# A mixture-of-experts stage whose row gathers are issued less far ahead: tokens four tiles instead of eight, results two token tiles instead of four, and additions spread more evenly over the steps

## The reference

```python
def _moe_forward(hidden_states, ...):                  # 1792 tokens x 256
    shared = einsum('ti,hi->th', silu(x @ sh_gate_w.T) * (x @ sh_up_w.T), sh_down_w)
    probs = softmax(x @ router_weight.T)
    top_v, top_i = top_k(probs, 2)
    ...
    for e in range(8):
        gate, up = split(x @ gate_up_proj[e].T)        # 176 columns each
        out = out + (silu(gate) * up @ down_proj[e].T) * combine[:, e:e + 1]
    return out + sigmoid(x @ shared_gate_w.T) * shared
x = _layernorm(x + attention(x))
x = _layernorm(x + cross_attention(x, ctx))
x = _layernorm(x + _moe_forward(x, ...))
```

## Time and profile before

| | |
|---|---|
| time, median of 3 runs | 1758.07 us (1757.87 to 1758.46) |
| span of the profiled execution, its own time | 1772.4 us |
| PE busy | 1696.6 us, 96% of the span |
| DVE, ACT, POOL busy | 1226.0, 932.4, 662.2 us |
| mean granted TensorE clock | 0.985 |
| chain that ended last | PE 77%, DVE 3%, DMA 3%, issue 2% |
| indirect fetches of tokens | 35, at 1608.7 to 1680.3 us |
| indirect gathers of results | 28, at 1708.5 to 1753.2 us |

### The profile page before, as it was taken

The page is one execution under the profiler, slowest core; times in us unless marked ns, Lnnn a source line. Parts: engine busy times, 40 slices in busy tenths (PEclk is TensorE's granted clock), DMA queues, the critical chain, the costliest instruction groups (busy, mean ns, idle before and its releaser), DMA issues.

```text
span 1772.4 us, 28874 instructions
## 1 busy us (share of the span) xinstructions
PE 1696.6 (96%) x10034; PEld 1525.3 (86%) x10034; DVE 1226.0 (69%) x3381; ACT 932.4 (53%) x1707; POOL 662.2 (37%) x417
## 2 busy tenths in 40 slices
PE   6999789999999999999999999999999999997986
PEld 6788678999898998989898989899898989887975
DVE  4555367777877768787777777776878787565446
ACT  4433246565656555565656565555556565543532
POOL 1111063333434435343333343443534331435334
PEclk9999999999999999999999999999999999999998
DMA  5133563333232324252333323233424221432322
GB/s 191 52 116 113 179 125 83 44 87 64 62 66 61 67 74 77 60 96 42 86 44 87 66 61 66 62 66 80 75 62 91 42 55 20 99 110 62 114 76 84
DMA packets 103000, 140.36 MB, mean 79 GB/s; under 512 B 37038, under 2 KB 81872, under 8 KB 102736
## 3 DMA queue, kind: packets, MB, share of 16 engines
q1 hardware_dynamic: 60928, 115.53, 27.3%
q10 hardware_dynamic: 38912, 14.80, 4.7%
q0 software_dynamic: 3024, 8.26, 1.7%
HBM read 113.68 MB, written 24.89 MB: 78 GB/s over the span
## 4 chain that ended last, share of the span: by engine, by line
PE 77%; DVE 3%; DMA 3%; issue 2%; ACT 1%; another core or an unknown queue 1%; POOL 0%; ACTq 0%; POOLq 0%; DVEq 0%; SPq 0%
PE b_turn L758 16%; PE b_out L775 9%; PE b_out L777 9%; PE b_out L776 9%; PE b_score L744 8%; PE b_score L746 8%; PE b_score L745 8%; PE b_out L785 5%; PE c_gate L1410 2%; DMA rden_store<-b_rden 2%; PE c_down L1437 1%; PE c_up L1424 0%; DVE c_up L1728 0%; DVE b_p L897 0%
## 5 line engine op out<-in xcount | busy, mean ns | idle before, releaser
L815 ACT CAST b_pT_hi<-b_turn 125x512 fp32r<-125x512 f32 (+1 forms) x768 | 406.3, 530 | 546.2 <-PE b_turn L758 543.8
L911 DVE TENSOR_TENSOR b_pT_lo<-b_turn,b_pT_hi 125x512 fp32r<-125x512 f32 (+1 forms) x768 | 477.8, 623 | 268.4 <-ACT b_pT_hi L815 262.9
L897 DVE CUSTOM_DVE_ANT_0 b_p<-b_score,b_mask_add 128x500 f32<-128x500 f32 x672 | 451.2, 673 | 56.6 <-PE b_turn L758 24.0
L758 PEld LDWEIGHTS b_turn<-ident,b_p 128*125 128x125 f32 x2688 | 409.9, 186 | 57.6 <-issue 1.1
L758 PE MATMUL b_turn<-ident,b_p 128*125 128x128 f32 x2688 | 418.5, 272 | 0.8 <-ACT b_p L821 0.8
L821 ACT ACTIVATE b_p<-b_p,b_shift 128x1500 f32<-128x1500 f32 x224 | 347.4, 1551 | 16.2 <-DVE b_top_min L905 8.3
L775 PE MATMUL b_out<-b_pT_hi,b_c_hi 125*128 125x512 f32 (+1 forms) x768 | 346.8, 452 | 7.2 <-DVE b_pT_lo L911 7.2
L1034 POOL TENSOR_TENSOR b_oT_lo<-b_oT,b_oT_hi 128x896 fp32r<-128x896 f32 x32 | 67.8, 2120 | 622.1 <-ACT b_oT_hi L843 622.1
L776 PE MATMUL b_out<-b_pT_lo,b_c_hi 125*128 125x512 f32 (+1 forms) x768 | 281.2, 366 | 0.0
L777 PE MATMUL b_out<-b_pT_hi,b_c_lo 125*128 125x512 f32 (+1 forms) x768 | 281.2, 366 | 0.0
L744 PE MATMUL b_score<-b_cT_hi,b_q_hi 128*128 128x500 f32 x672 | 264.6, 394 | 9.5 <-DVE b_cT_lo L984 9.5
(11 more groups left out here) (248 smaller groups left out, 2408.8 us busy)
## 6 DMA issues: line engine op xcount, KB each, us to landing
cT_in<-in_ctxT SPq DMA_DIRECT2D x32, 750.0 KB, 11.7
b_c_in<-in_ctx SPq DMA_DIRECT2D x32, 750.0 KB
q_store<-a_fold_in_or_q_stage SPq DMA_DIRECT2D x16, 896.0 KB, 4.0
q_in<-q_store SPq DMA_DIRECT2D x32, 448.0 KB, 8.2
b_rden_all<-rden_store ACTq DMA_DIRECT2D x32, 256.0 KB, 4.4
b_rden_all<-rden_store ACTq DMA_DIRECT2D x32, 192.0 KB, 4.6
b_mask_in<-in_mask SPq DMA_DIRECT2D x32, 187.5 KB, 10.7
slot_store<-c_y2T SPq DMA_DIRECT2D x35, 128.0 KB, 1.7
```

The costliest lines, as they stand in the source:

```text
L758: mm = pe.transpose(turn_bank[n % 3][0:CK, u * 128:(u + 1) * 128], p[slot % 2][:, u, c * CK:(c + 1) * CK], ident[:])
L815: act.copy(pT_hi[:, n % 3, 0:w], turn_bank[n % 3][0:CK, 0:w]).then_inc(hi_done, 1)
L897: dve.tensor_tensor_reduce(out=p[slot % 2][:, u, keys], in0=score_bank[j][:, 0:FW], in1=mask_add[:, b, keys], scale=1.0, scalar=-3.0e38, o ...
L911: dve.tensor_tensor(pT_lo[:, n % 3, 0:w], turn_bank[n % 3][0:CK, 0:w], pT_hi[:, n % 3, 0:w].bitcast(F32), ALU.subtract).then_inc(lo_done, 1)
```

## The change

A fetch now waits until the tile four before it is transposed, where it waited for the one eight before; there are still eight buffers. A gather now waits for the additions of the token tile two before it, where it waited for the one four before. The tuple of additions per step is (0, 1, 1, 1, 2, 1, 1, 2, 1, 1, 1, 1), where it was (0, 1, 1, 2, 2, 2, 1, 0, 1, 1, 1, 1); its sum stays 13, and the fourteenth addition follows the last step.

```diff
-        X_DEEP, Y_DEEP = 8, 4
+        X_DEEP, Y_DEEP, X_AHEAD, GATHER_AHEAD = 8, 4, 4, 2
...
-        COMBINE_AT = (0, 1, 1, 2, 2, 2, 1, 0, 1, 1, 1, 1)
+        COMBINE_AT = (0, 1, 1, 1, 2, 1, 1, 2, 1, 1, 1, 1)
...
             def fetch_x(s):
                 if s == 0:
                     pool.wait_ge(route_chain, SOURCED)
-                if s >= X_DEEP:
-                    pool.wait_ge(x_turned, s - X_DEEP + 1)
+                if s >= X_AHEAD:
+                    pool.wait_ge(x_turned, s - X_AHEAD + 1)
                 pool.indirect_dma_start(out=x_in[:, s % X_DEEP, :], out_offset=None, in_=D["y2"],
...
             def gather(k):
                 n = ORDER[k]
-                if k >= GATHERS:
-                    pool.wait_ge(added, 2 * (k - GATHERS + 1))
+                if k >= GATHER_AHEAD:
+                    pool.wait_ge(added, 2 * (k - GATHER_AHEAD + 1))
                 for j in range(2):
```

## The result

| | before | changed |
|---|---|---|
| time, median of 14 runs each | 1756.88 us (1754.39 to 1760.85) | 1761.22 us (1759.05 to 1765.19) |
| ratio | | 1.0025, 95% interval 1.0017 to 1.0033 |
| span of the profiled execution | 1772.4 us | 1757.5 us |

The change costs 4.3 us; 1755.6 had been forecast, a gain of 2.5. The time lies in the stated range, on the side of the slower rival. The profiled executions say the opposite of the timed ones: there the changed kernel is 14.9 us faster. A run's time is its span plus 1.8 us (1759.32 and 1757.5 for the changed kernel's profiled run), so the profiled execution of before stood for some 1774 us, and none of the timed runs of that kernel, then or later, was over 1763.65.

The account below looks back on a forecast made before the run. Bound by TensorE, with two holes (some 15 us) blamed on unbroken runs of indirect DMAs on GpSimd. Fetches -3.0, gathers and additions -5.3 + 4.8 + 1 = +0.5: -2.5 us, so 1755.6 us; range 1749 to 1764.

Parts of the forecast that it names:

- the slower rival: Step 17 to the end: holes don't come from the runs of DMAs, or timed runs lack them; 1766.8 or about 1763; chance 0.22.
- its two holes: TensorE's pauses near tile 9 of the routed stage and at 1720 to 1732 us, second shared stage; together some 15 us.
- Part 1, the fetches: Routed stage: fetches four ahead end their run earlier, so TensorE goes on sooner after tile 9; -3.0 us.
- Part 2, the order up to addition 5: Second shared stage: VectorE is the limit and addition 5 ends at 1731.4 instead of 1736.7; -5.3 us.
- Part 2, from addition 5 to the last three tiles: Second shared stage: a new chain over GpSimd takes 30.4 us where it was 25.6; +4.8 us.
- the three legs over GpSimd: Waits for gather 7 and a scale, gathers 9 and 10 and a scale, and gather 13: 6.1, 8.6 and 4.8 us.
- The tail: From addition 11's end to the last three tiles: 5.8 us where it was 3.7, 2.1 of the +4.8.
- +1 for the first six DMAs: Start of the gathers: the first six DMAs are still nearly one unbroken run, so some instruction starvation stays; +1 us.
- The rival of timed runs without holes: Variant of the slower rival: only the +4.8 and the old order's faster start count; about 1763; chance within its 0.22.
- so here it was not hidden: Near 1722 to 1732 us: no instruction-queue packets while TensorE crawled, taken as instruction loads kept waiting by gathers.

Follow-up runs that it names:

- the first profile: The kernel before, unchanged, in the profiled execution that the prediction read: span 1772.4 us, routed stage 99.84 us, second shared stage 53.77 us.
- e1: The kernel before, unchanged, run and profiled again: 1755.84 us, ratio 0.9997; profiled span 1755.3 us, second shared stage 46.68 us.
- e8: The kernel before with eight semaphores for gathers, so gathers run up to eight token tiles ahead instead of four: 1758.36 us, ratio 1.0008.
- e9: The kernel before, unchanged, profiled once more with one run: 1758.20 us; profiled span 1756.4 us.
- e10: The kernel before, unchanged, profiled yet again with one run: 1756.30 us; profiled span 1754.5 us.
- e2: The kernel before with only the fetches held to four tiles ahead; gathers and additions as before: 1756.24 us, ratio 0.9993.
- e5: The changed kernel with the scales of tiles 0 to 3 and 4 to 6 computed behind gathers 5 and 8 instead of 7 and 10: 1758.09 us, ratio 1.0015.
- e6: As e5, and the last two gathers wait for the additions four tiles before: 1756.55 us, ratio 1.0004 to the kernel before.
- e3: The kernel before with only the gathers held to two tiles ahead; fetches and additions as before: 1760.29 us, ratio 1.0016.
- e4: The kernel before with only the additions moved; fetches eight ahead, gathers four: 1759.38 us, ratio 1.0000.
- e7: The changed kernel with gathers three token tiles ahead instead of two: 1757.11 us, ratio 1.0003 to the kernel before.

## Why the prediction was wrong

**The step that failed is the first one**, "its two holes (together some 15 us) come from how far ahead GpSimd runs", and with it the assumption that they are there in every run. The observation was right: engines stood still, and the profile names nothing in the kernel that they waited for. The step from there to a lack of instructions was not: no run shows it, and the loads of the first profile lie where those of e1 lie. That the holes lay inside runs of DMAs doesn't show a cause: e1, e8, e9 and e10 have as long or longer runs without them. The number that spoke against it was in the table: the profiled span was 14.3 us over the median of runs that agreed within 0.6 us. I named this in a rival and gave it too little weight. The holes were as large as that difference, and this should have settled it.

**Part 1, the fetches: -3.0 forecast, 0 measured** (e2: 0.9993, interval to 1.0002; routed stage 92.06 against 92.50). That a fetch four ahead is early enough was right; the gain was the hole's. The sum had a slip as well: 2.3 us, the landing counted from the issue's end, was added to the start of the fetch at 1638.46. With the 3.26 us of the earlier trace rows its transfer ends at 1641.7 and that of fetch 13 at 1638.0, so silu 9 could have come some 0.4 us earlier, not 1.1.

**Part 2, the order up to addition 5: -5.3 forecast.** Counted from the first gather, addition 5 was forecast to end at 1731.4 - 1708.55 = 22.85 us. It ended at 1718.30 - 1695.52 = 22.78. That it fits to 0.07 us is partly luck: addition 1 ended 9.61 us after the first gather, not 9.34, and the walk from there took 13.17 us, not 13.5. The walk was sound; the thing it was compared with was not. In e1 the same addition ends 21.07 us after the first gather, not 28.15, so the term is **+1.7**: the addition now stands one step later in the program.

**Part 2, from addition 5 to the last three tiles: +4.8 forecast, +3.6 measured.** The chain was forecast at 30.4 us and took 1747.47 - 1718.30 = 29.17; in e1 it took 25.61, the 25.6 of the first profile. The holes of the first profile lay ahead of addition 5, so this stretch of it was sound. The 1.2 us too many lie nearly all in the three legs over GpSimd: 6.1, 8.6 and 4.8 us were forecast, and 5.6, 8.3 and 4.4 measured. ScalarE's waits, 2.2 and 3.2 us, came where they were put. The tail, "now 5.8" where it was 3.7, took 5.45 us and has VectorE wait 1.76 us for the last gather, and e5 and e6 show that scales and tail together are nearly all of the cost.

**+1 for the first six DMAs, "still nearly one run": 0.** No run shows such a term; the walk up to addition 5 came out without it.

With the right baseline the same walk gives 22.85 + 30.4 - 46.68 = +6.6 us, where the traces have +5.3 and the runs +4.3 (3.0 to 5.8 by the interval). The rival of timed runs without holes had put the time at about 1763; it came to 1761.22.

The Trainium skill (Runtime: NRT & Kernel Launch, section Instruction fetch mechanics) says that crossing a block of instructions is mostly hidden. The trace of e8 agrees, in which a load landed within a run of sixteen gathers without a pause, and so does the first profile, with its load at 1710 us. My "so here it was not hidden" did not follow: a window with no load in it doesn't show a load that stopped an engine.

## What to carry to other kernels

- Compare the profiled span with the timed runs before reading a stall in it. If the difference is as large as the stall, the profile shows an execution that isn't the one being timed: profile again before explaining it.
- Before a prefetch is held back, count what else stands behind it on its in-order queue. In the changed kernel the rows themselves were in time but for the first and the last gather; it was the small computation queued behind the gathers (1.6 us of work) that came late and held up ScalarE, and through it VectorE and TensorE. Moving it ahead won back 3.2 of 5.3 us. With the additions in their old steps (e3) the same queue made a gather's rows late instead.
- Look-ahead can have an edge: here three tiles cost nothing that shows (1.0003), two cost 0.25%. I read the edge, and this is not shown, as the point where issue and landing of a pair of gathers (2.5 us, and 3.3 from the second's issue), plus what is queued behind them, outgrow the steps until their use.

No version beat the kernel before. What TensorE still waits for in its second shared stage is VectorE, as e1's waits from 1690 us on show, and gathers eight ahead (e8: 1.7 and 1.8 us) don't change that:

```profile
PE c_up L1356 <- DVE c_h_lo L1734: 1.8, 2, 1.5
...
PE c_down L1376 <- DVE c_y L1750: 1.8, 1, 1.8
```

## What the runs showed of the hardware

In one of the twelve profiled executions of this study, ScalarE, VectorE and TensorE crawled at two places, for some 7 and some 10 us, with no wait in the program to account for it, and TensorE's granted clock fell to the lower of its two levels in both (1640.0 to 1646.8 and 1725.3 to 1735.6 us). Against e1 the two stages took 7.3 and 7.1 us longer. The cause stays open.

The clock also fell in executions without a hole. In the second shared stage it was at its lower level for 6.8 us in the changed kernel, behind TensorE's wait of 3.1 us, and for 3.4 us in e1 (from 1731.6 us), behind one of 1.8; in e4, e6 and e7 it fell only within the stage's last 1 us. What this costs no run separates: in the changed kernel's chain TensorE has no part there, in the chains of e3 and e9 it has.

Back-to-back indirect DMAs, one of 128 rows every 1.25 us, go on beside full matmul streams without slowing them: in e1 a tile took 2.1 to 2.5 us from tile 9 on, beside them as after them.
